# Scan and experts on one core: POOL leaves group 5 at state 12, group 6 sums into its own PSUM bank, out projections are spread anew

## The reference

```python
# mamba: d_inner 512, 16 states
xz = xn @ in_proj_w.T;  x, z = split(xz)
x = silu(causal_conv4(x) + conv_b)
dt, B, C = split(x @ x_proj_w.T);  dt = softplus(dt @ dt_proj_w + 2 * dt_proj_b)
h[t] = exp(dt * A) * h[t-1] + dt * B * x            # for each of 16 states
y = (sum over states of h * C + x * D) * z
mamba = y @ out_proj_w.T
# experts: 64 of inner size 128, top 8 of a softmax for each token
moe = sum over chosen e of p_e * (silu(xn @ g_e.T) * (xn @ u_e.T)) @ w2_e.T
```

## Time and profile before

| | |
|---|---|
| timed runs | 499.99, 503.32, 513.6 us |
| profiled execution | 495.79 us, span 494.0 us |
| PE busy | 410.0 us, 83% |
| PEld busy | 299.1 us, 61% |
| DVE busy | 432.0 us, 87% |
| ACT busy | 248.2 us, 50% |
| POOL busy | 327.0 us, 66% |
| chain that ended last (DVE, PE, issue) | 10%, 8%, 1% of the span |

### The profile page before, as it was taken

How to read it: one execution, slowest core, us unless ns; L and a number is a source line. 1 busy time by engine, 2 the same in 40 slices (tenths; PEclk the granted TensorE clock), 3 DMA queues, 4 the chain that set the end, 5 groups by cost and what they waited for, 6 DMA issues and landing times. The chain is left out here.

```text
span 494.0 us, 8730 instructions
## 1 busy us (share of the span) xinstructions
PE 410.0 (83%) x2094; PEld 299.1 (61%) x2094; DVE 432.0 (87%) x651; ACT 248.2 (50%) x469; POOL 327.0 (66%) x281
## 2 busy tenths in 40 slices
PE   1986989018859999899999998899989849865997
PEld 1732434002229888788978886788878735533675
DVE  5297999989997998999889997999899899999984
ACT  1245269132335566566666674556656522554560
POOL 2000578777767788878865665878877687778770
PEclk9997899655558999999999998999999988995999
DMA  8999389962234999999999996999999663333331
GB/s 274 428 425 426 138 297 400 407 244 106 101 144 159 347 376 374 354 322 357 346 365 329 338 359 234 347 340 353 363 349 336 247 202 93 101 113 105 113 117 53
DMA packets 51849, 134.39 MB, mean 272 GB/s; under 512 B 7120, under 2 KB 11216, under 8 KB 49776
## 3 DMA queue, kind: packets, MB, share of 16 engines
q1 hardware_dynamic: 45680, 117.31, 65.1%
q0 software_dynamic: 6144, 16.79, 10.3%
HBM read 90.49 MB, written 45.68 MB: 276 GB/s over the span
## 5 line engine op out<-in xcount | busy, mean ns | idle before, releaser
L344 POOL TENSOR_TENSOR dbu<-dtu,bc 128x512 f32 x80 | 102.7, 1286 | 57.3 <-DVE bank L600 46.4
L336 POOL DMA_INDIRECT slot_x<-x_sb,slot x64 | 69.3, 1082 | 68.5 <-DMA slot_x<-bc 49.3
L600 DVE TENSOR_TENSOR_SCAN bank<-dA,dbu 128x512 f32<-128x512 f32 x68 | 92.6, 1362 | 8.9 <-POOL dbu L344 1.3
L786 ACT ACTIVATE dA<-dt_sb,a_neg 128x512 f32<-128x512 f32 (+1 forms) x68 | 49.2, 725 | 68.2 <-DVE bank L600 68.1
L600 DVE TENSOR_TENSOR_SCAN bank<-bank,dbu 128x512 f32<-128x512 f32 x60 | 73.7, 1229 | 5.3
L1034 PE MATMUL bank<-x_sb,wring 128*128 128x128 f32 x528 | 67.9, 284 | 0.0
L606 DVE TENSOR_TENSOR hc<-bank,bc 128x512 f32<-128x512 f32 x90 | 61.8, 687 | 5.2 <-POOL hp L354 3.2
L1034 PEld LDWEIGHTS bank<-x_sb,wring 128*128 128x128 f32 x528 | 65.0, 200 | 0.3
L1034 PE MATMUL bank<-x_sb,xw 128*128 128x128 f32 x512 | 62.6, 275 | 0.7 <-DMA xw<-w_moe 0.7
L1034 PEld LDWEIGHTS bank<-x_sb,xw 128*128 128x128 f32 x512 | 59.7, 192 | 1.2 <-issue 1.2
L786 ACT ACTIVATE bank<-dt_sb,a_neg 128x512 f32 x60 | 41.6, 693 | 35.1 <-DVE bank L600 35.0
(11 more groups left out here) (175 smaller groups left out, 735.8 us busy)
## 6 DMA issues: line engine op xcount, KB each, us to landing
xw<-w_moe SPq DMA_DIRECT2D x64, 384.0 KB, 5.4
wring<-w_moe SPq DMA_DIRECT2D x64, 384.0 KB, 5.4
slot_y<-x_sb SPq DMA_DIRECT2D x66, 256.0 KB, 5.5
slot_x<-bc SPq DMA_DIRECT2D x16, 1024.0 KB, 21.9
bc<-bc_dram SPq DMA_DIRECT2D x8, 1024.0 KB, 15.5
xg<-slot_x SPq DMA_DIRECT2D x16, 512.0 KB, 6.0
xw<-slot_x SPq DMA_DIRECT2D x16, 512.0 KB, 6.1
slot_y<-w_moe SPq DMA_DIRECT2D x1, 2048.0 KB, 13.7
```

The source lines that it names most:

```text
L336: pool.indirect_dma_start(slot_x, bass.IndirectOffsetOnAxis(ap=slot[:, t * K + k:t * K + k + 1], axis=0), x_sb[:, t, :], None).then_inc(sc ...
L344: nc.gpsimd.tensor_tensor(dbu[:, j], at(dtu, g), bc[:, bass.ds(n, 1), 0].rearrange("p a l -> p (a l)"), ALU.mult).then_inc(dbu_ok, 1)
L600: nc.vector.tensor_tensor_scan(H[:], dA[:, j] if fall is None else fall, dbu[:, j], 0.0, ALU.mult, ALU.add).then_inc(scan_ok, 1)
L786: nc.scalar.activation(dA[:, j] if fall is None else fall, at(dt_sb, g), ACT.Exp, scale=a_neg[:, bass.ds(g, 1), bass.ds(n, 1)].rearrange(" ...
```

## The change

There are five edits.

1. POOL leaves group 5 at state 12 (`ALONE = NS - 4`). For states 12 to 15 VectorE spreads u itself, one state ahead, and writes the products to four buffers of their own (`hc_alone`); TensorE sums these four singly instead of taking POOL's last quad. Group 5 is written out behind the loop on POOL and VectorE.
2. Group 6 sums into bank 1 (`acc_of`), which held decays before. Its first sum waits for the last scan of group 5 (`scan_ok`), and the first sum of group 7, again in bank 0, waits only for the read-out of group 5 (`min(g + 1, G2 + 1)`).
3. The read-out of group 6 moves back on VectorE by two states, behind state 5 of group 7.
4. The table `PROJ` and the banks `OUT` of the output tiles are new, with their waits.
5. Bacc is asked for 8192 bytes of descriptor scratch per partition (default 16384), which makes room for the new buffer `extra`. That buffer and the function `ahead` serve spreads that POOL could do between gathers; `PAUSE` is empty, so none is done.

```diff
-        OUT = [PS[i][:, 0:DM] for i in (4, 5, 6, 7, 1, 2, 4, 5)]
+        OUT = [PS[i][:, 0:DM] for i in (4, 5, 6, 7, 2, 4, 5, 6)]
...
-        PROJ = {9: (4, 0), 11: (4, 1), 13: (5, 0), 15: (5, 1), 21: (6, 0), 23: (6, 1), 25: (7, 0), 26: (7, 1),
-                27: (4, 2), 28: (5, 2), 29: (6, 2), 30: (7, 2)}
+        PROJ = {9: (4, 0), 10: (4, 1), 20: (5, 0), 21: (5, 1), 24: (6, 0), 25: (6, 1), 26: (4, 2), 27: (5, 2),
+                28: (7, 0), 29: (7, 1), 30: (6, 2), 31: (7, 2)}
+        def acc_of(g):
+            return PS[1] if g == G2 else Y_ACC
+        ALONE = NS - 4
+        PAUSE = {}
...
-            with pool.Fori(DT, G2) as g:
+            with pool.Fori(DT, G2 - 1) as g:
                 with pool.Fori(0, QG // 2) as q:
                     pairs(g, q)
-            add_pair((G2 - G1) * QG - 1, 1)
+            with pool.Fori(0, ALONE // 4) as q:
+                pairs(G2 - 1, q)
+            r = (G2 - 1 - G1) * QG + ALONE // 2 - 1
+            add_pair(r, 1)
...
-            def light(g, p):
+            def light(g, p, alone=False):
...
                         scan(g, n, k % 2, dA_light(n))
+                        if alone and ALONE - 1 <= n < NS - 1:
+                            spread_u(g, n + 1, 1 - k % 2)
...
+                        if own:
+                            if n == NS - 1:
+                                dve.wait_ge(hq_ok, (G2 - G1) * (NS // 4))
+                            times_c(g, n, k % 2, hc_alone)
+                        else:
+                            if k % 2 == 0:
+                                dve.wait_ge(hp_ok, (g - G1) * QG + n // 2 + 1)
+                            times_c(g, n, k % 2)
...
-            pair0(G3, 0, 2 * NS, hc_end)
-            pair0(G3, 1, 2 * NS, hc_end)
-            finish_group(G2)
+            for q in range(3):
+                tail_pair(G3, q)
+            finish_group(G2, acc_of(G2))
...
-                if n == 0:
-                    pe.wait_ge(y_out, g + 1)
-                mm = nc.tensor.matmul(Y_ACC[:], ident[:], ring[n % len(ring)], start=(n == 0), stop=True, skip_group_check=True)
+                if n == 0 and g == G2:
+                    pe.wait_ge(scan_ok, G2 * NS + C)
+                elif n == 0:
+                    pe.wait_ge(y_out, min(g + 1, G2 + 1))
+                mm = nc.tensor.matmul(acc_of(g)[:], ident[:], ring[n % len(ring)], start=(n == 0), stop=True, skip_group_check=True)
...
-            sum_quad((G2 - G1) * (NS // 4) - 1)
+            for n in range(ALONE, NS):
+                sum_states(G2 - 1, n, hc_alone, 1)
...
-                        if t >= 6:
-                            pe.wait_ge(cb_out, t - 5)
-                        else:
-                            pe.wait_ge(row_ok[t - 4], NS + 1)
+                    if k == 0 and t >= 5:
+                        pe.wait_ge(cb_out, t - 4)
...
-    nc = bacc.Bacc("TRN2", target_bir_lowering=False, num_devices=1)
+    nc = bacc.Bacc("TRN2", target_bir_lowering=False, num_devices=1, dynamic_dma_scratch_size=8192)
```

More of the change, by code:

```diff
@@ L389, in _ @@
                 for k in range(K):
+                    for g, n in PAUSE.get(t * K + k, ()):
+                        ahead(g, n)
                     pool.indirect_dma_start(
@@ L594, in spread_u, with scan @@
                                         ALU.mult).then_inc(dbv_ok, 1)
-            def scan(g, n, j, fall=None):
+            def scan(g, n, j, fall=None, given=None):
                 s = g * NS + n
@@ L607, in times_c, with finish_group @@
                                         ALU.mult).then_inc(hc_ok, 1)
[L609 removed]
+            def finish_group(g, bank=None):
                 dve.wait_ge(acc_ok, (g + 1) * NS + C)
[L612 removed]
+                nc.vector.scalar_tensor_tensor(at(u_g, g), at(u_g, g), at(d_col, g), (bank or Y_ACC)[:], ALU.mult, ALU.add).then_inc(y_out, 1)
                 dve.wait_ge(y_out, g + 2)
@@ L699, in _, with tail_pair @@
             dve.wait_ge(row_ok[1], NS + 1)
-            with dve.Fori(GH + 1, G2) as g:
+            with dve.Fori(GH + 1, G2 - 1) as g:
                 light(g, (g - GH - 1) * LIGHT + V_LAST)
+            light(G2 - 1, (G2 - GH - 2) * LIGHT + V_LAST, alone=True)
             hidden(PAIRS, 0)
+            def tail_pair(g, q):
+                for j in range(2):
+                    n = 2 * q + j
+                    if n % PART == 0 and (n >= RING or g == G3):
+                        dve.wait_ge(acc_ok, g * NS + n - RING + PART + C)
+                    s = (g - G2) * NS + n
+                    if (g, n) in BY_POOL:
+                        i = BY_POOL.index((g, n))
+                        dve.wait_ge(dbu_ok, DBU_MOE + i + 1)
+                        scan(g, n, j, given=extra[:, i % 4])
+                    else:
+                        dve.wait_ge(dbv_ok, NS + NS - ALONE + s + 1 - sum((h - G2) * NS + m < s for h, m in BY_POOL))
+                        scan(g, n, j)
+                    after = (g, n + 1) if n < NS - 1 else (g + 1, 0)
+                    if after[0] < G and after not in BY_POOL:
+                        spread_u(after[0], after[1], 1 - j)
+                    times_c(g, n, j, hc_end)
             spread_u(G2, 0, 0)
-            dve.wait_ge(hp_ok, (G2 - G1) * QG + 1)
+            dve.wait_ge(hp_ok, (G2 - G1) * QG - 2 + 1)
             dve.wait_ge(t_ok, PAIRS)
-            pair0(G2, 0, NS, hc_end)
-            pair0(G2, 1, NS, hc_end)
+            for q in range(2):
+                tail_pair(G2, q)
             finish_group(G2 - 1)
-            for q in range(2, QG - 1):
-                pair0(G2, q, NS, hc_end)
-            pair0(G2, QG - 1, NS, hc_end, (G3,))
-            pair0(G3, 0, 2 * NS, hc_end)
-            pair0(G3, 1, 2 * NS, hc_end)
-            finish_group(G2)
-            for q in range(2, QG - 1):
-                pair0(G3, q, 2 * NS, hc_end)
-            pair0(G3, QG - 1, 2 * NS, hc_end, ())
+            for q in range(2, QG):
+                tail_pair(G2, q)
+            for q in range(3):
+                tail_pair(G3, q)
+            finish_group(G2, acc_of(G2))
+            for q in range(3, QG):
+                tail_pair(G3, q)
             finish_group(G3)
```

24 lines of the change are left out of this document (16 added, 8 removed).

## The result

The changed kernel took 508.65 us (median of 508.34, 508.61, 508.69 and the profiled 511.96), 9 us over the forecast and outside its range. The kernel before, timed beside it, took 499.99, 503.32, 511.24 and 513.6 us. Executions of either kernel that fell in a slower state of the chip, here the 511.24 and 513.6, are left out of every ratio. The ratio is then 1.0151 with an interval of 1.0076 to 1.0226: 0.8 to 2.3% slower, where I had forecast a gain of 2 us.

What follows compares the result with a forecast made beforehand. VectorE, then TensorE, idle 8.79 us for group 6's read-out, set the end. VectorE's end 481.33 plus tail 10.61 gave span 491.94, 2.1 below 494.0; 501.66 less 2.1 gave 499.6 us, range 492.5 to 507.

Steps and rivals of the forecast that it cites:

- I cost this at nothing: POOL's gathers starting near 386.8 instead of 397.10 us: nobody waits for the earlier start, so 0 us.
- rival of a collision: Early gathers overlap the last expert weight loads near 391 us, delaying TensorE: +1.3 us net, span 495.3; chance 0.14.
- I take 0, since three in flight is far from any limit: Halved descriptor scratch on POOL: 0 us taken, with 2 to 3 us possible in the scatter before the experts.
- The middle of the four is 501.66: Base of the timed forecast: middle of the kernel before's four times; less 2.1 gives 499.6 us.
- A gain of 3.3 us: Group 6 in its own bank, projections spread anew: with VectorE's end unmoved, span 490.70 us instead of 494.0.
- finish of group 7: On VectorE near the end: follows about 1.3 us behind the last product instead of 4.77 us idle.
- fixed tail: From VectorE's last product to the span's end, mostly TensorE's remaining work: 10.61 us.
- first tail scan: VectorE's scan at the tail's start, no longer beside POOL's addition, falls from 2.02 to 1.23 us: -0.79.
- The four states alone: VectorE works group 5's last four states: four spreads add 2.36 us, two vanished waits give -0.45.
- granted clock: TensorE in the tail: priced at full clock, 1.00 granted beyond 430 us.
- slower rival of a held clock: TensorE's clock stays at the lower level through group 7: about 22 us, span 514, 4% slower; chance 0.04.

Runs made afterwards that it cites:

- late_8k: The changed kernel (8192 bytes of scratch) with the gathers waiting for VectorE's last hidden step; ratio to the kernel before 1.0071 [1.0016, 1.0126].
- late_16k: The changed kernel with default scratch and gathers waiting for VectorE's last hidden step; span 505.4, four times 504.9 to 518.49, no ratio.
- late_16k_b: late_16k run again, on one chip with after_again; ratio to the kernel before 0.9967 [0.9927, 1.0006].
- before_again: The kernel before, unchanged, recorded once more; span 498.1, tail 92.41.
- thin: The changed kernel with default scratch, its first 16 gathers fetching rows of 32 numbers instead of 256; span 488.7, one time of 490.44.
- bank_only: The kernel before plus only the accumulator bank, new projection table and later read-out of group 6, default scratch; ratio 1.0033 [0.9994, 1.0072].
- bank_only_b: bank_only run again, on one chip with after_again; ratio to the kernel before 1.0035 [0.9997, 1.0073].
- before_8k: The kernel before with the descriptor scratch halved to 8192 bytes and nothing else; ratio 1.0036 [0.9981, 1.0091].
- no_gathers: The kernel before without its 64 gathers (semaphores raised, experts' part of output missing), on the quiet chip; ratio 0.9992 [0.9971, 1.0013].
- pause_t2: bank_only with the 17th gather waiting for the scan of state 10 of group 6, on the quiet chip; ratio 0.999 [0.9961, 1.0019].
- after_again: The changed kernel, unchanged, run in a later set; ratio to the kernel before 1.0136 [1.0087, 1.0186].

## Why the prediction was wrong

**The step that failed most: "I cost this at nothing" (gathers earlier).** I asked whether the gathers would be late, and whether they would take bytes from the weight loads. I did not ask what an unbroken row of 16 indirect DMAs does to engines that still have work of the experts in hand. Beside it ScalarE's last tanh stood 11.45 us, and through it VectorE's entry into the tail. Taking only the early start away takes the stall away (late_8k, and with the default scratch late_16k, late_16k_b); halving the row cuts it to 3.17 us; an eighth of the bytes leaves it. My rival of a collision had the right place and the wrong mechanism and price: the first product near 391 waited for no weights, and 1.3 us net became 11.5. I also missed a wait: the 17th gather asks for the last down projection, whose weights lie in its buffer, so POOL stood 6.38 us there, once the tanh was late.

What within the chip holds ScalarE is open. Shown is when it ends (with the row of gathers), what it does not depend on (the bytes, the scratch), and that it was absent in the one trace with early gathers from the quiet chip. So the early gathers are needed for it but do not suffice; what the chip adds is not known.

The Trainium skill ("DMA: Bandwidth & Descriptors", section "Queues, rings and completion order"), which I had set beside the collision, says that a DMA engine takes turns between queues that have work. No weight load was late here, so that rule bore on the smaller question; what was held is an instruction that moves no data by DMA.

**"I take 0, since three in flight is far from any limit" (scratch).** Wrong, and past my upper bound of 2 to 3 us: 2.61 to 7.00 us at the 57th scatter. I had looked at the gathers' pace and not at the 64 scatters, and at DMAs in flight where what counts is how many fit before the first wrap. The same page of the Trainium skill says in its sections "Terms" and "SWDGE vs HWDGE vs iDMA" that POOL appends descriptors to rings in SBUF and that a descriptor is a struct of 16 bytes. As an estimate from that page, made after the fact, 8192 bytes hold 512 of them, and if a DMA takes 8 rows and one completion of each ring, 56 DMAs use 504; the 57th is the first that does not fit. The traces agree on the 57th in four of four. But by the same estimate the default fills at the 114th DMA, the 50th gather, and no trace has POOL idle there. So the estimate gives the place and not the wait: why it is of several us, with the early DMAs long landed, and why it does not come again, no run shows.

**The base.** "The middle of the four is 501.66": I knew that the profiled execution was the fastest and corrected for it by a number only. What differed was a mechanism: a typical execution has 8 us of stalls in the tail (before_again 92.41 against 84.21), the profiled one had none. Against the two medians of before, 503.32 and 507.28, even a right sum would have come out 2 to 6 us higher. The forecast gain has one faint sign on record: thin, on the quiet chip, took 490.44 us where before took 493.35 to 497.42. It is a single time, of a kernel whose first two tiles are wrong.

**"A gain of 3.3 us" from the bank.** The mechanism was right: TensorE's 8.79 us of idle time are gone, finish of group 7 follows the last product by 1.28 us of idle time (forecast 1.3), fixed tail 10.86 us (10.61). But the gain exists only where TensorE comes in late. In before_again VectorE's stalls let it catch up, and the rest is 10.76 us with the old bank. bank_only and bank_only_b at 1.003 each say the same.

**Right in size.** The first tail scan took 1.23 us as forecast. The four states alone: late_8k, late_16k and late_16k_b have a stage of 250.1 to 250.3, six with POOL's help (before, before_again, before_8k, bank_only, no_gathers, pause_t2) 246.8 to 249.4, mean 247.9, so +2.3 us against the 1.9 of 2.36 - 0.45 (+1.2 with the scan). The tail shrank by 1.14, of which 0.79 is the first scan. The granted clock stood at 1.00 beyond 440 us, with TensorE busy 15.82 to 17.48 of 20 us, so the slower rival of a held clock falls. The dip to 0.66 between 400 and 420 belongs to the stall: TensorE had 4.22 us of work in those 20.

**The range.** It was built from a spread of runs and a sum whose zeros had no upper end. The gathers' step had a rival of +1.3 us and the scratch 2 to 3, and both were exceeded.

## What to carry to other kernels

When an edit moves a series of software-issued DMAs next to other engines' last dependent work, don't cost it by bytes or lateness alone: make one variant that holds the series back by a semaphore, and compare. Count the DMAs between start and first pause before you shrink their scratch. Record the kernel before twice: a gain that rests on one engine's lag in one trace may be gone in the next.

## What the runs showed of the hardware

- With 8192 bytes of descriptor scratch POOL stalls at its 57th indirect DMA of 128 rows, by 2.61 to 7.00 us (four traces); with 16384 never among 64.
- A back-to-back row of 16 indirect gathers (one per 1.25 us) went with one ScalarE instruction standing 11.45 to 14.45 us with its inputs ready, in seven traces on at least four chips, one of them with an eighth of the bytes; not in the one trace on the quiet chip, where the kernel before ran 1.6% faster (median 494.99 against 503.27 on the chip of after_again).
- On four chips TensorE has stretches of 5 to 12 us in which its instructions start 0.7 us or a multiple of it apart, without any releaser in the profile (before_again 433.6 to 442.0, late_16k 480.1 to 489.9). Where one stood between 25 and 15 us before the end, the rest was 20.98 us against some 10.9 without (late_16k).
